# Fetching every 60th group of three tiles row by row from SyncE, in the second layer of a graph network

## The reference

```python
src = node_embeds[rows]; tgt = node_embeds[cols]       # rows = src, cols = dst
q = (src @ Wq.T + bq).reshape(-1, 8, 16)
k = (tgt @ Wk.T + bk).reshape(-1, 8, 16)
v = (tgt @ Wv.T + bv).reshape(-1, 8, 16)
exp_att = exp(clip(einsum('ehd,ehd->eh', q, k) / 4, -10, 10))
out = segment_sum((exp_att / (segment_sum(exp_att, rows)[rows] + 1e-8))[..., None] * v, rows)
```

## Time and profile before

| | us |
|---|---|
| median of the runs | 6205.74 |
| profiled execution, its own time | 6258.93 |
| its span, first to last instruction | 6257.2 |
| busy in the span: PE / PE weight loads | 3015.3 / 2368.1 |
| busy: DVE / ACT / POOL | 3094.1 / 1816.7 / 3185.1 |
| mean granted TensorE clock | 0.615 of full speed |

### The profile page before, as it was taken

The page is one execution under the profiler, slowest core; times in us unless marked ns, Lnnn a source line. Parts: engine busy times, 40 slices in busy tenths (PEclk is TensorE's granted clock), DMA queues, the critical chain, the costliest instruction groups (busy, mean ns, idle before and its releaser), DMA issues. The chain is left out here.

```text
span 6257.2 us, 86473 instructions
## 1 busy us (share of the span) xinstructions
PE 3015.3 (48%) x21028; PEld 2368.1 (38%) x21028; DVE 3094.1 (49%) x8514; ACT 1816.7 (29%) x5489; POOL 3185.1 (51%) x3338
## 2 busy tenths in 40 slices
PE   4445445445445445344465555554554545445453
PEld 3323323333333233233243444444444444444442
DVE  6536445445445445344244555555555555555556
ACT  3233332333332333333443222222222222222222
POOL 4364464464463464554535555555555555555554
PEclk8555555556556555555557666666666666666666
DMA  2231231231222221222322222222222222222223
GB/s 80 54 82 47 64 82 46 67 79 48 70 74 50 73 73 49 76 70 62 73 54 75 76 75 75 76 76 76 76 76 76 76 76 75 76 76 75 75 76 56
DMA packets 205061, 436.91 MB, mean 70 GB/s; under 512 B 67172, under 2 KB 114781, under 8 KB 204606
## 3 DMA queue, kind: packets, MB, share of 16 engines
q0 software_dynamic: 153968, 371.50, 22.4%
q1 hardware_dynamic: 49934, 59.56, 3.4%
q10 hardware_dynamic: 704, 0.33, 0.0%
HBM read 415.27 MB, written 55.69 MB: 75 GB/s over the span
## 5 line engine op out<-in xcount | busy, mean ns | idle before, releaser
L525 POOL DMA_INDIRECT got<-hk_table,dst x1563 | 1523.3, 975 | 1513.1 <-PE bank L1000 821.5
L1486 POOL DMA_INDIRECT kv<-kv_table,dst_i x1611 | 1527.0, 948 | 1287.6 <-DVE wv_s L1528 846.8
L766 DVE TENSOR_TENSOR acc<-acc,bank 128x129 f32 x2187 | 635.3, 290 | 1480.8 <-remote 737.7
L1633 PE MATMUL bank<-q,ohT 128*128 x4833 | 617.9, 281 | 934.5 <-ACT ohT L1585 834.0
L998 PE MATMUL bank<-got,oh 128*128 x2187 | 616.9, 285 | 794.5 <-issue 445.1
L1644 PE MATMUL bank<-wv_s,oh_f 128*128 128x136 f32 x3222 | 768.5, 397 | 463.9 <-DVE wv_s L1528 249.8
L1507 DVE TENSOR_TENSOR prod<-bank,kv 128x384 f32<-128x384 f32 x537 | 297.7, 554 | 1271.6 <-remote 1042.3
L1633 PEld LDWEIGHTS bank<-q,ohT 128*128 128x128 bf16 x4833 | 481.7, 121 | 1035.1 <-issue 985.8
L1644 PEld LDWEIGHTS bank<-wv_s,oh_f 128*128 128x128 f32 x3222 | 635.2, 279 | 536.0 <-DVE wv_s L1528 297.9
L1579 ACT ACTIVATE oh_f<-oh 128x384 f32<-128x384 bf16 x537 | 279.6, 521 | 1683.0 <-remote 1235.2
L1101 ACT ACTIVATE oh<-away 128x384 bf16<-128x384 bf16 x733 | 383.8, 524 | 1311.5 <-remote 788.0
(11 more groups left out here) (223 smaller groups left out, 3409.3 us busy)
## 6 DMA issues: line engine op xcount, KB each, us to landing
slots_by_bin<-sorted_chunk SPq DMA_DIRECT2D x637, 61.0 KB
kv<-kv_table,dst_i POOLq DMA_INDIRECT x1611
got<-hk_table,dst POOLq DMA_INDIRECT x1563
kv_table<-qkv SPq DMA_DIRECT2D x12, 512.0 KB, 2.9
hk_table<-hk POOLq DMA_DIRECT2D x6, 772.0 KB, 5.7
out<-o SPq DMA_DIRECT2D x12, 256.0 KB
xs<-in_x SPq DMA_DIRECT2D x3, 768.0 KB, 10.7
sorted_chunk<-vT SPq DMA_DIRECT2D x13, 64.0 KB
```

The lines of the kernel that those rows point to most:

```text
L525: g.indirect_dma_start(out=got[:, (tile0[k] + t) % RING0, :], out_offset=None, in_=hk_d, in_offset=bass.IndirectOffsetOnAxis(dst0[:, k % 2 ...
L766: v.tensor_tensor(out=o, in0=o, in1=bank[5 + u % 3][:, i * W0:(i + 1) * W0], op=ALU.add)\
L1486: g.indirect_dma_start(out=kv[:, r, i, :], out_offset=None, in_=kv_d, in_offset=bass.IndirectOffsetOnAxis(dst_i[:, t:t + 1], 0))\
L1633: ins = t.matmul(bank[2 + u % 2][:, i * D:(i + 1) * D], ohT[:, u % 2, i * P:(i + 1) * P], q3[:, bass.ds(regs[0][(s + i) % REGS], 1), j * D ...
```

## The change

`by_row` is the list of every 60th group: 59, 119, 179, 239, 299, 359, 419 and 479. These 8 groups are no longer gathered by POOL. SP fetches them, one DMA of one row (1 KB) per edge: 8 x 384 = 3072 DMAs. Their target is a tile of its own, `rows_in`, with two slots. SP loads the addresses into registers, 24 at a time (six TENSOR_LOADs for a tile of 128 edges, so 18 for a group), from `nat` itself, which is for that turned into integers and masked in place by two more DVE instructions in the middle part. SP starts at the beginning of the loop and waits only, from the third of its groups on, for the `weigh` of the group that used the slot before. POOL's ring of 8 slots is counted over the remaining 529 groups. The computation is the same.

```diff
+ROW_EVERY = 60
+ROW_LOT = 24
@@ vector, middle part, behind slots_of
+                ends = nat[:, :, :].bitcast(I32)
+                c.inc(v.tensor_copy(ends, nat[:, :, :]))
+                after(v, c)
+                c.inc(v.tensor_scalar(out=ends, in0=ends, scalar1=8191, scalar2=None, op0=ALU.bitwise_and))
@@ the loop
+        by_row = [u for u in range(GROUPS) if u % ROW_EVERY == ROW_EVERY - 1]
+        lot_of = [u - u // ROW_EVERY for u in range(GROUPS)]
+            @block.sync
+            def _(sp):
+                for x, u in enumerate(by_row):
+                    if x >= 2:
+                        sp.wait_ge(s_wgh, by_row[x - 2] + 1)
+                    for i in range(G):
+                        s = u * G + i
+                        row = dst_n[s % P:s % P + 1, s // P, :]
+                        for a, b in pieces(P, ROW_LOT):
+                            _, numbers = nc.values_load_multi_w_load_instructions(
+                                row[:, a:b], engines=[mybir.EngineType.SP], min_val=0, max_val=NODE_SLOTS - 1,
...
+                            for e in range(a, b):
+                                sp.dma_start(rows_in[e:e + 1, x % 2, i, :], kv_d[bass.ds(numbers[e - a], 1), :])\
+                                  .then_inc(s_row1[x % 2], 16)
@@ gpsimd
+                    if u in by_row:
+                        continue
+                    r = lot_of[u] % RING1
@@ vector, product(u)
+                    if u in by_row:
+                        x = by_row.index(u)
+                        v.wait_ge(s_row1[x % 2], 16 * G * P * (x // 2 + 1))
+                    else:
+                        v.wait_ge(s_gk[lot_of[u] % RING1], 16 * G * (lot_of[u] // RING1 + 1))
```

More of the change, by code:

```diff
@@ L1462, in build, with kv_of @@
         wv_s = sbp(phase, "wv_s", [P, 2, G, W], FP32)
+        by_row = [u for u in range(GROUPS) if u % ROW_EVERY == ROW_EVERY - 1]
+        lot_of = [u - u // ROW_EVERY for u in range(GROUPS)]
+        rows_in = sbp(phase, "rows_in", [P, 2, G, 2 * D], FP32)
+        dst_n = nat[:, :, :].bitcast(I32)
+        s_row1 = [sem(f"s_row1_{x}") for x in range(2)]
+        def kv_of(u):
+            return rows_in[:, by_row.index(u) % 2, :, :] if u in by_row else kv[:, lot_of[u] % RING1, :, :]
         s_i1 = sem("s_i1")
@@ L1477, in build @@
         with nc.Block() as block:
+            @block.sync
[9 more added lines that the diff above has]
+                                row[:, a:b], engines=[mybir.EngineType.SP], min_val=0, max_val=NODE_SLOTS - 1,
+                                skip_runtime_bounds_check_because="13 bits of an edge's end, drawn below the number of nodes")
+                            for e in range(a, b):
+                                sp.dma_start(rows_in[e:e + 1, x % 2, i, :], kv_d[bass.ds(numbers[e - a], 1), :])\
+                                  .then_inc(s_row1[x % 2], 16)
             @block.gpsimd
@@ L1480, in _ @@
                 for u in range(GROUPS):
-                    r = u % RING1
-                    if u >= RING1:
-                        g.wait_ge(s_wgh, u - RING1 + 1)
+                    if u in by_row:
+                        continue
+                    r = lot_of[u] % RING1
+                    if lot_of[u] >= RING1:
+                        g.wait_ge(s_wgh, max(w for w in range(u) if w not in by_row
+                                             and lot_of[w] == lot_of[u] - RING1) + 1)
                     for i in range(G):
@@ L1505, in product @@
                     v.wait_ge(s_q, u + 1)
-                    v.wait_ge(s_gk[u % RING1], 16 * G * (u // RING1 + 1))
+                    if u in by_row:
[3 more added lines that the diff above has]
+                        v.wait_ge(s_gk[lot_of[u] % RING1], 16 * G * (lot_of[u] // RING1 + 1))
                     v.tensor_tensor(out=prod[:, u % 2, :, :],
                                     in0=bank[2 + u % 2][:, 0:G * D].rearrange("p (g f) -> p g f", f=D),
-                                    in1=kv[:, u % RING1, :, 0:D], op=ALU.mult).then_inc(s_prod, 1)
+                                    in1=kv_of(u)[:, :, 0:D], op=ALU.mult).then_inc(s_prod, 1)
                 def reduce(u):
@@ L1528, in weigh @@
                     v.tensor_tensor(out=by_head(wv_s[:, u % 2, :, 0:D]),
-                                    in0=by_head(kv[:, u % RING1, :, D:2 * D]),
+                                    in0=by_head(kv_of(u)[:, :, D:2 * D]),
                                     in1=weight.unsqueeze(3).to_broadcast([P, G, HEADS, HEAD_DIM]),
```

## The result

| | us |
|---|---|
| before, median of 4 runs | 6210.54 |
| changed, median of 4 runs | 6297.06 |
| ratio, 95% interval | 1.0142, 1.0117 to 1.0167 |
| loop before, first to last `product` (profile) | 6186.3 - 3362.4 = 2823.9 |
| loop after, unrounded difference | 2876.6 (3339.6 to 6216.1) |

The account below looks back on a forecast made before the run. It took a limit cycle of gathers and pauses, 5.27 us per gathered group, to bound the kernel. Eight waits of 94 us (+752) less 21 saved gave +731 on 6205.7, say 6930 us; range 6340 to 7440 us.

Parts of the forecast that it names:

- The limit cycle and the engines that stand while gathers fly: Loop: nine gathers, then a pause; engines but POOL nearly stand while many gathers fly; 5.27 us per gathered group.
- turns of 15.8 us between them: Loop, sign of being right: between DVE's waits for SP's rows, turns of three groups still last 15.8 us.
- SP's time for a group, undisturbed, 287 us: SP in the loop: 384 rows at 0.68 us (261 us) plus 18 register loads (26 us) per group.
- What the gathers leave of it, 0.62: Loop: SP's effective share of its undisturbed pace beside gathers, taken between 0.57 and 0.68.
- disturbed throughout: Rival, loop: SP takes 2.8 us a row whenever gathers are issued, share 0.46, +1131 us, 7337 us; chance 0.17.
- The sum for each group, 94 us of wait: Loop: SP does 193 of 287 us in time; DVE waits the other 94 in `product`, 8 times, 752 us.
- Saved, 21 us: Loop: 24 gathers of 8 groups go, 5.27 us a group, of which 2.7 remain: 8 x 2.6 = 21 us.
- The middle part: Two added DVE instructions, about 1.3 us each, covered by 6.68 us of DVE idle time: cost nothing.
- cheap rows: Rival, SP's rows in the loop: work 237 us, share 0.68, 26 us wait per group, +187, 6393 us; chance 0.15.
- SP keeps up: Rival, loop: gathers don't hold SP, `product` never waits, -21 to -42 us, 6164 to 6185 us; chance 0.13.
- One engine: Rival, SP's one-piece copies: each waits for the last's landing on one DMA engine, +5376, about 11600 us; chance 0.05.

Follow-up runs that it names:

- e4: The kernel before, unchanged, run and profiled once more for scatter: median 6257.23 us, loop 2818.5 us.
- e6: Changed kernel with every 30th group fetched by SP instead of every 60th (17 groups, 6528 rows): ratio 1.2734 against the kernel before.
- e8: Kernel before, POOL gathering all groups, plus 3072 unused one-row SP DMAs at fixed addresses, no register loads; the stream ends in mid-loop: ratio 0.9960.
- e7: Changed kernel with each row DMA laid out over 16 pieces of 16 numbers instead of one piece: 6937 us, ratio 1.1087 against the kernel before.
- e3: The changed kernel, unedited, run and profiled once more for scatter: median 6364.85 us, ratio 1.0169 against the kernel before.
- e1: Changed kernel with the 8 groups neither gathered nor fetched (a tile of zeros, no wait): ratio 0.9963 against the kernel before, -23 us.
- e2: Changed kernel with POOL gathering all 537 groups again and SP's 3072 row DMAs going to an unread tile: ratio 0.9937 against the kernel before, -42 us.
- e10: As e8, but 6912 unused fixed-address row DMAs instead of 3072, meant to last the whole loop: ratio 0.9917 against the kernel before.
- e9: Changed kernel with every 72nd group fetched by SP instead of every 60th (7 groups, 2688 rows): 6149 us, ratio 0.9895 against the kernel before.

## Why the prediction was right and wrong

*The limit cycle and the engines that stand while gathers fly*: right for the kernel before, and again in e4. The sign "turns of 15.8 us between them" failed: beside SP's stream the turns are mostly of six gathers and 9.7 us.

*SP's time for a group, undisturbed, 287 us*: wrong, and the step that failed. It measured 185 us, and all of the difference is in the rows: 0.41 us each and not 0.68 (157 us, not 261), while the register loads took 28 us for the 26 I gave them. The 179 us in the expectations of e6 count each load at 1.2 us, the median of all. I took the pace of L466, which has 16 pieces, for that of one piece, and bounded it from below by 237 us with a static DMA of 0.389 us. The bound was not a bound but a single instance: other static DMAs on SP's queue were shorter in the same trace, and e8's static rows take 0.252. The line in the trace of before:

```profile
L425 SPq DMA_DIRECT2D rows<-tile_bases x13: 298/308/318, 40.8 to 2439.3; - x13
```

e7 is the test: with 16 pieces the row costs 0.69 us, and with its loads (15 x 1.46 + 3 x 0.54) the work is 288 us, what I forecast for the change. That e7's median is also the forecast time, 6937 us, is luck: it is 678 us above before on its chip, from waits of 76 us and not 94 and from ordinary steps that are 87 us longer in all, which I had not forecast.

*What the gathers leave of it, 0.62*: too high, and for another reason than mine. SP did 185 - 22 = 162 us of its work in the 59 x 5.07 = 299 us without a wait, a share of 0.54 (0.52 in e3). That is 23 us a group, as much as the whole measured wait. Its rows are disturbed for as long as gathers are issued, as the rival "disturbed throughout" had it, but cost 1.17 us there and not 2.8. The 2.8 came from small DMAs beside the gathers of the first part, and didn't carry over to the loop. With an addition of some 0.8 us to either row the share depends on the row: (288 - 76) / (59 x 5.43) = 0.66 in e7.

*The sum for each group, 94 us of wait*: measured 22.4 and, in e3, 29.5. From 94, the work takes off 102, the lower share gives back 23 and the shorter time between the groups (299 us, not 311) 7: 22. This closes by construction, as the share is worked out from the wait; the test of the form is e6, forecast from another run's figures and met within 6 us at twice the density. A difference of two like terms takes all the error of both: a third less of work left a quarter of the wait.

*Saved, 21 us*: wrong by a term that I put at nothing. The removed gathers give 20 us in the sum (23 us in e1's total). The ordinary steps give 106 more, and e2, e8 and e10 show that SP's stream alone shortens them (68 us in e2's loop against e4's). That they do it by turns of six gathers instead of nine is what the trace shows beside it, and not a full account: e7 has the sixes and longer steps. I had asked only whether the stream disturbs the others, never whether it could help them.

*The middle part*: right. The two instructions take 1.02 and 1.03 us, and DVE is still idle for 4.72 us behind them.

*The rivals*: "cheap rows" had the right term and still too dear a row. "SP keeps up" fell with the 8 waits. e9, with 12 more groups of distance, has its outcome and is faster than before, but not its mechanism: SP still needs some 340 us for a group beside the gathers. "One engine" fell: the rows follow one another at 0.41 us. The Trainium skill, "DMA: Bandwidth & Descriptors", gives a fixed cost of about 2 us in its section "Anatomy of one DMA", for a DMA issued from GpSimd. With a row every 0.41 us, such a cost can't be the pace of this stream: if the rows had it, they overlapped. No run here shows on how many DMA engines they went.

## What to carry to other kernels

When an engine's queue is to do work beside a loop, compare its undisturbed time with the distance between deadlines and again with its time beside the loop's traffic; here 185 us undisturbed, 299 + 3 us of distance and 349 us beside the traffic, and twelve groups more of distance (with seven such groups instead of eight) turned a loss of 1.4% into a gain of 1.0%. Price a DMA's issue by a row with the same number of pieces, and where the trace has none, let the range go well below the nearest row. A change that adds a stream of small transfers can shift the phase of a loop that swings between bursts and pauses, either way (here steps of 5.07 us with rows of one piece and 5.43 with rows of 16, from 5.27), so leave the work out and keep the stream (or the reverse) before explaining a sum.

## What the runs showed of the hardware

- SP issues a one-row DMA of 1 KB with its address in a register every 0.408 us (DMA 0.225 us), in 16 pieces every 0.69 us (0.506 us), and with a fixed address every 0.295 us (0.252 us), with no gather beside it. A TENSOR_LOAD of 24 numbers takes 1.71 us there, one of 8 numbers 0.79 (1.46 and 0.54 in e7).
- While GpSimd's gathers are in flight a row of SP's takes 0.76 to 0.80 us more in the mean with either register form, and only 0.14 us more (0.436 against 0.295 us) with a fixed address, a form with one instruction instead of three.
- A stream of 1 KB DMAs in one piece on SP's queue makes this kernel faster by 0.4% (3072 DMAs in 1207 us) to 0.8% (6912 DMAs in 2603 us) without doing any of its work. The bursts are mostly of six gathers and not nine while it lasts, and grow again at once behind it (e8). In 16 pieces (e7) they are of six too, but the turn takes 11.4 us and not 9.7, and the steps are longer than without a stream. Why the standing engines go on sooner in the one case stays open, and so does why a turn takes longer in the other.
